# Inter-chunk states of a linear attention kept as 128x128 blocks instead of 64-column ones

## The reference

```python
xn = _layernorm(x)                                  # x: (8, 1024, 128), 8 batches
# linear attention: 16 heads of 8, chunks of 64 tokens
qkv = (xn @ W_qkv).reshape(B, L, 3, H, DK)
k = _layernorm_noaffine(k)                          # over the 8 elements of a head
def step(S, chunk):                                 # S: (B, 16, 8, 8)
    inter = einsum('bhde,bthe->bthd', S, q_c)
    scores = where(causal, einsum('bthd,bshd->bhts', q_c, k_c), 0.0)
    intra = einsum('bhts,bshd->bthd', scores, v_c)
    S = S + einsum('bthd,bthe->bhde', v_c, k_c)
    return S, inter + intra
attn = y.reshape(B, L, 128) @ W_o
# mixture of 8 experts, each token goes to the one with the largest xn @ centroids.T
h = relu(einsum('etd,efd->etf', layernorm(xn) * ln_g + ln_b, w1) + b1)
y_e = xn + einsum('etf,edf->etd', h, w2) + b2
gated = a * y_e + (1 - a) * xn                      # a = sigmoid(xn @ centroids.T)
out = x + attn + sum(onehot * gated)
```

## Time and profile before

| | |
|---|---|
| median of 3 runs | 363.04 us (362.52 to 364.0) |
| the profiled execution | 363.22 us, its span 361.4 us |
| granted TensorE clock | 0.99 of full speed |
| PE busy | 341.2 us, 94% |
| PEld busy | 293.5 us, 81% |
| DVE busy | 283.6 us, 78% |
| ACT busy | 241.7 us, 67% |
| POOL busy | 250.2 us, 69% |

### The profile page before, as it was taken

The page is one execution under the profiler, slowest core; times in us unless marked ns, Lnnn a source line. Parts: engine busy times, 40 slices in busy tenths (PEclk is TensorE's granted clock), DMA queues, the critical chain, the costliest instruction groups (busy, mean ns, idle before and its releaser), DMA issues. The chain is left out here.

```text
span 361.4 us, 17478 instructions
## 1 busy us (share of the span) xinstructions
PE 341.2 (94%) x6868; PEld 293.5 (81%) x6868; DVE 283.6 (78%) x799; ACT 241.7 (67%) x657; POOL 250.2 (69%) x245
## 2 busy tenths in 40 slices
PE   7799999989899999999999989999999999999990
PEld 7466776777587787777877878999999999999990
DVE  8887898898785988977878786788887778877760
ACT  4788677777667657666665735766677667766660
POOL 3388567889886865455455503888887888888884
PEclk9999999999999999999999999999999999999996
DMA  7403213021433233255233225555555555555420
GB/s 203 103 22 92 63 38 86 26 77 54 128 98 92 91 93 91 82 149 152 93 99 100 78 58 137 69 72 72 68 64 77 72 76 67 70 75 61 37 23 0
DMA packets 46705, 28.99 MB, mean 80 GB/s; under 512 B 5096, under 2 KB 44320, under 8 KB 46624
## 3 DMA queue, kind: packets, MB, share of 16 engines
q1 hardware_dynamic: 34352, 19.34, 19.6%
q0 software_dynamic: 12272, 8.54, 17.1%
HBM read 14.53 MB, written 13.78 MB: 78 GB/s over the span
## 5 line engine op out<-in xcount | busy, mean ns | idle before, releaser
L495 POOL DMA_INDIRECT out_dram<-qx,rows x71 | 112.7, 1588 | 36.0 <-issue 21.9
L695 ACT ACTIVATE qx<-sc,b1T 128x128 f32<-128x128 f32 x280 | 79.8, 368 | 40.4 <-PE sc L1424 40.4
L421 POOL DMA_INDIRECT slots_d<-rows,pos_i x64 | 62.8, 981 | 41.3 <-PE bank L1331 10.7
L857 DVE TENSOR_TENSOR pr<-sc,causal 128x1536 f32<-128x1536 f32 (+2 forms) x33 | 63.5, 1926 | 16.3 <-PE sc L1277 16.2
L1432 PE MATMUL bank<-tokens,qx 128*128 128x128 f32 x568 | 75.2, 276 | 0.7 <-ACT qx L695 0.7
L1424 PE MATMUL sc<-wide,tokens 128*128 128x128 f32 x560 | 74.1, 275 | 0.4 <-issue 0.4
L1432 PEld LDWEIGHTS bank<-tokens,qx 128*128 128x128 f32 x568 | 69.0, 192 | 1.1 <-ACT qx L695 1.1
L1424 PEld LDWEIGHTS sc<-wide,tokens 128*128 128x128 f32 x560 | 68.2, 192 | 0.6 <-issue 0.6
L1016 DVE COPY tokens<-xT 128x1024 f32 x71 | 53.3, 752 | 0.2 <-issue 0.2
L1277 PEld LDWEIGHTS sc<-qx,kT 32*64 32x64 f32 x2048 | 32.9, 130 | 16.8 <-issue 16.4
L1031 DVE SCALAR_TENSOR_TENSOR qx<-bank,rows,qx 128x128 f32<-128x128 f32 x71 | 24.8, 350 | 27.2 <-PE bank L1432 26.5
(11 more groups left out here) (167 smaller groups left out, 531.4 us busy)
## 6 DMA issues: line engine op xcount, KB each, us to landing
rows<-slots_d SPq DMA_DIRECT2D x71, 66.0 KB, 2.0
out_dram<-tokens SPq DMA_DIRECT2D x16, 256.0 KB, 2.7
tokens<-in_L_attn_x_dram SPq DMA_DIRECT2D x7, 512.0 KB, 4.2
w1raw<-in_L_ffn_w_dram SPq DMA_DIRECT2D x8, 256.0 KB, 3.3
w2raw<-in_L_ffn_w_dram SPq DMA_DIRECT2D x8, 256.0 KB, 2.9
out_dram<-qx,rows POOLq DMA_INDIRECT x71, 3.4
slots_d<-rows,pos_i POOLq DMA_INDIRECT x64
slots_d<-empty SPq DMA_DIRECT2D x9, 66.0 KB
```

What stands on the lines that cost most here:

```text
L421: pool.indirect_dma_start(slots_d, bass.IndirectOffsetOnAxis(ap=pos_i[:, t:t + 1], axis=0), rows[:, t, :], None)\
L495: pool.indirect_dma_start(out_rows, bass.IndirectOffsetOnAxis(ap=xs[:, a, D + 2:D + 3].bitcast(U32), axis=0), ye[:, a, :], None, bounds_ch ...
L695: last = nc.scalar.activation(ht[:, k % 2, c * P:(c + 1) * P], inner(k)[:, c * P:(c + 1) * P], ACT.Relu, bias=b1T[:, bass.ds(e * FC + c, 1)])
L857: nc.vector.tensor_tensor(pr[:, h % 2, a:G, w].rearrange("p g (j t) -> p g j t", t=CH), sc[:, a * BANK:G * BANK].rearrange("p (g w) -> p g ...
```

## The change

`state`, `smid` and `dstate` hold 128 columns per tile instead of 64. `state_step` issues the same sixteen 64x64 matmuls, but writes the two blocks of a tile to the diagonal of a 128x128 block, so that a tile has 128 columns and the four fill a bank. The masking multiplies all 512 columns with `headmask`, which zeroes what lies off the diagonal (values left over in the bank); `smask` goes. The additions run over 512 columns too. `inter_first` and `inter_second` issue four matmuls with all 128 rows and 128 weight columns, over 64 moving columns, in place of eight.

The bank FA has no columns left for the ranks. They move to Y[0] (`RANKS`), and with them their place: `rank_tokens` comes behind the query projection of n = 3, 5, 7, 9 and waits for the result of quad n - 1 (which reads Y[0]), and `ranks`, `places` and `tiles_of_experts` come behind `result` on VectorE. For this the output of quad 8 becomes early (`out_early`: n < 11). The affinities and the state step of the quad behind wait for `rank_sb`, which the query projection did before.

`affT` lies in `sq`; ScalarE's square of k waits for the transposes of the affinities. `ln_b` and `b2` swap places, and `ln_b` is loaded at n = 4 instead of 6.

```diff
-        b2b = tokens[:, 0:E * D].rearrange("p (e d) -> p e d", d=D)
-        lbb = tokens[:, CW:CW + E * D].rearrange("p (e d) -> p e d", d=D)
+        lbb = tokens[:, 0:E * D].rearrange("p (e d) -> p e d", d=D)
+        b2b = tokens[:, CW:CW + E * D].rearrange("p (e d) -> p e d", d=D)
...
-        state = sb("state", [P, B, GW])
-        smid = sb("smid", [P, HALF, GW])
-        dstate = sb("dstate", [P, NC, HALF, GW])
-        smask = sb("smask", [P, GW])
+        state = sb("state", [P, B, D])
+        smid = sb("smid", [P, HALF, D])
+        dstate = sb("dstate", [P, NC, HALF, D])
...
-        affT = sb("affT", [P, HALF * P])
+        affT = sq
...
-        RANK = HALF * GW
+        RANKS = Y[0]
...
-            return n % 2 == 1 and n < 9
+            return n % 2 == 1 and n < 11
...
-                if n == 6:
+                if n == 4:
                     stored(n - 1)
                     sp.dma_start(lbb, ln_b.partition_broadcast(P)).then_inc(s("lb_in"), 16)
...
             def k_square(n):
                 act.wait_ge(s("kn_sb"), n + 1)
                 reach(act, s("kvar_ready"), n)
+                reach(act, s("aff_ps"), min(NB, max(0, n - 1) // 2))
...
-                nc.vector.tensor_tensor(dstate[:, 0, :, :], Y[n % 2][:, 0:HALF * GW].rearrange("p (i k) -> p i k", k=GW),
-                                        bcast(smask[:, :], 1, HALF), ALU.mult).then_inc(s("dsta_sb"), 1)
+                nc.vector.tensor_tensor(dstate[:, 0, :, :], Y[n % 2][:, :].rearrange("p (i k) -> p i k", k=D),
+                                        bcast(headmask[:, :], 1, HALF), ALU.mult).then_inc(s("dsta_sb"), 1)
...
                         dstate_first(n)
                     if n < NQ - 2:
                         dstate_second(n)
-                    if n in (3, 5, 7, 9):
-                        ranks(n // 2 - 1)
                     if n >= LATE:
                         state_steps(n)
...
-                    if n in (3, 5, 7, 9):
-                        places(n // 2 - 1)
-                    if n == LATE:
-                        tiles_of_experts()
...
                     if n and out_early(n):
                         result(n - 1)
+                    if n in (3, 5, 7, 9):
+                        ranks(n // 2 - 1)
+                        places(n // 2 - 1)
+                    if n == LATE:
+                        tiles_of_experts()
...
             def q_project(n):
-                if n in (4, 6, 8, 10):
-                    pe.wait_ge(s("rank_sb"), n // 2 - 1)
...
-                if n in (3, 5, 7, 9):
-                    rank_tokens(n // 2 - 1)
                 for i in range(HALF):
                     for a in range(P // GW):
                         for c, bank in ((0, Y[n % 2]), (1, FA))[:2 if n < NQ - 2 else 1]:
                             r, k = slice(CH * c, CH * (c + 1)), slice(i * D + GW * a, i * D + GW * (a + 1))
-                            last = mm(bank[GW * a:GW * (a + 1), i * GW:(i + 1) * GW], kn[r, n % 2, k], vp[r, k], start=True,
-                                      stop=True)
+                            last = mm(bank[GW * a:GW * (a + 1), k], kn[r, n % 2, k], vp[r, k], start=True, stop=True)
...
                     for i in range(HALF):
-                        for a in range(P // GW):
-                            r = slice(GW * a, GW * (a + 1))
-                            last = mm(Y[half][r, i * P:i * P + CH], state[r, half * HALF + i, :],
-                                      qT[r, half, i * P:i * P + CH], start=(i == 0), stop=False)
+                        last = mm(Y[half][:, i * P:i * P + CH], state[:, half * HALF + i, :], qT[:, half, i * P:i * P + CH],
+                                  start=(i == 0), stop=False)
...
                 for i in range(HALF):
-                    for a in range(P // GW):
-                        r = slice(GW * a, GW * (a + 1))
-                        last = mm(Y[half][r, i * P + CH:(i + 1) * P], smid[r, i, :], qT[r, half, i * P + CH:(i + 1) * P],
-                                  start=False, stop=False)
+                    last = mm(Y[half][:, i * P + CH:(i + 1) * P], smid[:, i, :], qT[:, half, i * P + CH:(i + 1) * P],
+                              start=False, stop=False)
...
                 pe.wait_ge(s("counted"), b + 1)
+                pe.wait_ge(s("res_ready"), 2 * b + 3)
...
                     if more:
                         q_project(n + 1)
+                    if n in (3, 5, 7, 9):
+                        rank_tokens(n // 2 - 1)
```

More of the change, by code:

```diff
@@ L813, in _ @@
             ln_norm(1, (6, 7))
-            nc.vector.tensor_reduce(out=smask[:, :], in_=headmask[:, :].rearrange("p (g k) -> p k g", k=GW), axis=AX,
-                                    op=ALU.add)
             def kT_copy(n):
@@ L964, in ranks @@
                 if b == NB - 1:
[L966 to L967 removed]
+                    link(nc.vector.tensor_scalar(cnt_i[:, :], RANKS[:, BATCH * E:BATCH * E + E], float(P - 1), None, ALU.add))
+                nc.vector.tensor_tensor(rank[:, :, :], RANKS[:, 0:BATCH * E].rearrange("p (t e) -> p t e", e=E),
                                         ohb[:, b * BATCH:(b + 1) * BATCH, :], ALU.mult).then_inc(s("rank_sb"), 1)
@@ L1286, in bank_y_free @@
                     pe.wait_ge(s("aff_sb"), n // 2)
+                if n % 2 == 0 and 4 <= n <= 10:
+                    pe.wait_ge(s("rank_sb"), n // 2 - 1)
             def inter_first(n):
@@ L1353, in rank_tokens @@
                 if b == NB - 1:
-                    last = mm(FA[:, RANK + BATCH * E:RANK + BATCH * E + E], onesb[:, :], total[:, NT - 1, :], start=True, stop=True)
+                    last = mm(RANKS[:, BATCH * E:BATCH * E + E], onesb[:, :], total[:, NT - 1, :], start=True, stop=True)
                 last.then_inc(s("rank_ps"), 1)
```

10 lines of the change are left out of this document (5 added, 5 removed).

## The result

The changed kernel takes 379.82 us in the median of 4 runs (378.89 to 381.22), the kernel before 363.38 (362.52 to 364.0) on the same chip: ratio 1.0458, with a 95% interval of 1.0427 to 1.049. That is 16.4 us slower. Forecast were 374.2 and a range to 377.5: the sign is right, the size is 5.2 us short. The profiled execution took 380.02 us with a span of 378.3 (before: 363.22 and 361.4), so the two traces differ by 16.8 and can stand for the medians. The attention part now ends 17.07 us later, and the expert part behind it has kept its length.

What follows compares the result with a forecast made beforehand. TensorE's queue in the attention part, and its waits for other engines, was taken as the bound. Sets 5.0, VectorE 5.7 and ranks 0.5 summed to +11.2 us on 363.2: 374.4, or 374.2 as median; range 370 to 377, with rivals 366.5 to 377.5.

Steps and rivals of the forecast that it cites:

- Sets on TensorE: Full-height inter-chunk sets in attention take longer than the 64x64 ones: +5.4 us, counted as 5.0 because n = 5 swallows 0.36.
- Rival 1: Weight load hidden, sets at the old pace (0.5 us), VectorE's additions stay: 366.9 us; chance 0.13.
- VectorE in n = 0: The query projection of n = 0 waits for two longer VectorE instructions: +0.54 us.
- VectorE in n = 9: Longer operations and two round trips delay the scaled values; w2 transposes start 2.85 later, 0.45 of it the sets': +2.4 us.
- GpSimd: Additions of 512 elements, +0.6 us each, two a period up to n = 8, covered by slack: costed at nothing.
- Rival 3: GpSimd becomes the bound in n = 4 to 6, late masks and longer rank round trips: +2.6, 377 us; chance 0.10.
- VectorE in n = 3, 5, 8, 10 to 15: TensorE waits for VectorE: +0.27 in n = 3, 8, 11, 15, +0.81 in 5, +0.3 in 10, 13, +0.25 in 14.
- Four operations at +0.27: Four VectorE state lines go from 256 to 512 elements a partition: +0.27 us each, 12 us of VectorE in all.
- Ranks: Rank matmuls behind the query projection are now open on TensorE: +0.2, +0.2, +0.1 for n = 3, 5, 7, together 0.5 us.

Runs made afterwards that it cites:

- e3: Changed kernel with state, smid and dstate 64 wide and full-height sets reading a constant matrix, ranks still moved: 373.17 us, ratio 1.0259.
- e1: Changed kernel with the old state layout, 64-column states and 64x64 sets, so only ranks and order are moved: 368.32 us, ratio 1.0139.
- e2: Changed kernel with the inter-chunk sets undone to eight 64x64 matmuls, vector operations still 512 wide and ranks moved: 376.28 us, ratio 1.036.
- e4: Changed kernel with nine unused 128x128 transposes filling TensorE's wait ahead of the query projection of n = 0: 376.66 us, ratio 1.0358.
- e5: Changed kernel with nine filling transposes in n = 0, plus eight ahead of the w1 and eight ahead of the w2 transposes of n = 9: 375.98 us.
- e6: Changed kernel with ranks(3), places(3) and tiles_of_experts of n = 9 behind VectorE's scaling of the values of n = 10: 377.03 us, ratio 1.0361.
- e7: Changed kernel with GpSimd's additions to smid and state narrowed to 256 elements a partition from n = 2 on: 375.89 us, ratio 1.0309.
- e11: Kernel before with places(3) and tiles_of_experts of n = 9 moved behind the scaling of the values: 362.67 us, ratio 0.9976.
- e14: Kernel before with places(3) and tiles_of_experts late in n = 9, and 64 already-met semaphore waits added on TensorE: 363.46 us, ratio 0.9992.
- e12: Kernel before with places(3) and tiles_of_experts late in n = 9, and four norm statistics ahead of ln_shift and ln_norm in every even h: 363.48 us.

## Why the prediction was right and wrong

- **Sets on TensorE, +5.4, 5.0 net: right.** 0.83 and 0.94 us a set against 0.86 and 0.96; alone they are worth 4.9 (e3 less e1) or 3.5 beside wide operations (changed less e2). Rival 1's 0.5 us a set is refuted.
- **VectorE in n = 0, +0.54: right, and incomplete.** "Two longer instructions, +0.54" is what the start moved by. What the longer idle time does to the clock behind it had no term, a step that failed by being left out: 2.6 us in the three groups, of which the period gives back 2.2 when the clock stays (e4). The forecast asked what is late next and not at which clock it runs.
- **VectorE in n = 9, +2.4: right** (2.9 with the sets in that period, measured 2.9 up to the w2 transposes); the 1.1 above it is the clock again (e5). e6 takes n = 9 back by 3.6 us in all. The forecast missed that ScalarE's queue carries the delay on to qT.
- **GpSimd, "I cost it at nothing": the step that failed by its reasoning.** It asked only whether GpSimd's results come too late, and found slack, which is there. e7 shows 2.0 us all the same, and its rows point to another way: GpSimd's longer additions hold up VectorE's small operations with two inputs in SBUF (nmr 553 ns, in e7 166). It was to be read before: 347 ns in the mean for a 128x8 operation in the line shown above, where e7 has 166. Rival 3 was near in size and had the wrong mechanism. The Trainium skill ("GPSIMD Engine Reference", section "1. Specifications") states this contention for VectorE's instructions with two SBUF inputs; the trace agrees, with 1.34 against 0.28 us.
- **VectorE in n = 3, 5, 8, 10 to 15: about right.** From n = 10 on 3.3 measured against 3.4. In n = 1 to 8 the 2.5 that are missing are GpSimd's 2.0 and a remainder of 0.5 that stays open. Four operations at +0.27 were right as prices, and 11.2 of VectorE's 17.3 us more of work are theirs; most of the rest is the held-up small operations.
- **Ranks, +0.5 in n = 3, 5, 7: about right.** Each adds 0.25 and the query projection 0.08 more.

Sum: 11.2 + 2.2 and 1.1 of clock + 2.0 by GpSimd = 16.5, against 17.07 in the traces; 0.3 in n = 0 and 0.5 in n = 1 to 8 stay open, and n = 10 to 15 were forecast 0.1 too high. So two terms that the forecast put at nothing failed: the clock behind a lengthened wait of TensorE (3.3 us), and GpSimd's longer additions (2.0 us). The first is in part luck of the execution, since the same wait kept the clock in the trace of e6; but none of the changed kernel's four executions had a mean clock above 0.983. The range ended at 377.5, because its bounds held each named term and no term for either.

## What to carry to other kernels

Where a change lengthens a wait of TensorE, add to the wait what the clock may cost behind it (here 2.2 us for one longer by 0.5), and fill the idle time with transposes nobody reads. Where it widens a GpSimd operation, look at which VectorE operations with two SBUF inputs lie beside it and compare their slowest with their fastest instance. Where a variant differs by 1 to 2 us and TensorE stands in mid-group on "issue", shift the program by a few dozen instructions before believing the difference.

## What the runs showed of the hardware that I had not expected

- TensorE at 1.2 GHz behind waits of 0.75 and 1.05 us in one trace, and at 2.4 GHz behind the same waits in another (e6). The mean clock is 0.992 in the trace of the kernel before, which kept it through the attention part, and 0.975 to 0.983 in the four executions of the changed kernel.
- TensorE at 1.2 GHz right behind a hole in its own instructions, in e2 (2.11 us), e11 (2.52) and e14 (2.31); in e12 the clock stayed behind one of 2.29.
- One VectorE instruction on 128x128 takes 0.28 us or 1.34 us, by what GpSimd does.
- Holes of up to 2.5 us in TensorE's own instruction stream at fixed records of the program, movable in steps of 16 records for 64 waits.
